# Loading the hashed rows with four DMAs a half, and turning them into dense columns

## What is computed

```python
xk = x + dxprev * time_maa_k
e_idx = token_ids.reshape(N).astype(jnp.int32) * HASH_PRIME % E
...
buf = jnp.zeros((E * C + 1, D), dtype=x.dtype).at[slot].set(xk_flat)
expert_in = buf[:E * C].reshape(E, C, D)
h = jnp.square(jax.nn.relu(jnp.einsum('ecd,edf->ecf', expert_in, w_key)))
expert_out = jnp.einsum('ecf,efd->ecd', h, w_value)
```

## Time and profile before

| | us |
|---|---|
| median of 3 runs | 2495.83 (2494.95 to 2498.03) |
| the profiled execution's own time | 2494.64 |
| its span in the profile | 2492.9 |
| hashed experts, from the first turn to the last product | about 1471 to 1852 of the span |
| granted TensorE clock, mean of the span | 0.993 |

### The profile page before, as it was taken

The page is one execution under the profiler, slowest core; times in us unless marked ns, Lnnn a source line. Parts: engine busy times, 40 slices in busy tenths (PEclk is TensorE's granted clock), DMA queues, the critical chain, the costliest instruction groups (busy, mean ns, idle before and its releaser), DMA issues.

```text
span 2492.9 us, 40630 instructions
## 1 busy us (share of the span) xinstructions
PE 2429.3 (97%) x12307; PEld 2021.7 (81%) x12309; DVE 1195.2 (48%) x1833; ACT 901.0 (36%) x1459; POOL 548.4 (22%) x498
## 2 busy tenths in 40 slices
PE   8999999999999899999999989999999999999999
PEld 4778888888899688888888868888888888888877
DVE  5555455325343243443444357777753333333356
ACT  3233333216555322222222236666652222222234
POOL 1100000002222266666666610000001111111100
PEclk9999999999999899999999999999999999999999
DMA  8698888407466533364345256666642111111135
GB/s 287 203 336 301 304 320 312 164 18 275 164 214 248 178 114 115 109 254 120 106 126 178 93 197 223 235 242 225 233 171 77 51 44 45 51 46 46 42 101 185
DMA packets 165172, 420.68 MB, mean 169 GB/s; under 512 B 31379, under 2 KB 67699, under 8 KB 148578
## 3 DMA queue, kind: packets, MB, share of 16 engines
q1 hardware_dynamic: 137810, 322.08, 37.2%
q0 software_dynamic: 19072, 61.66, 8.1%
q10 hardware_dynamic: 8208, 35.88, 3.8%
HBM read 558.71 MB, written 144.80 MB: 282 GB/s over the span
## 4 chain that ended last, share of the span: by engine, by line
PE 68%; DMA 2%; DVE 2%; issue 2%; ACT 1%; SPq 0%; POOL 0%; another core or an unknown queue 0%; DVEq 0%; POOLq 0%; ACTq 0%
PE s_g L99 8%; PE s_g L101 8%; PE s_g L100 8%; PE s_h_ps L99 5%; PE s_h_ps L101 5%; PE s_h_ps L100 5%; PE s_z_ps L99 2%; PE s_z_ps L101 2%; PE s_z_ps L100 2%; PE s_o_ps L99 2%; PE s_o_ps L100 2%; PE s_o_ps L101 1%; PE s_h L99 1%; PE s_h L100 1%; PE s_h L101 1%
## 5 line engine op out<-in xcount | busy, mean ns | idle before, releaser
L99 PE MATMUL s_g<-wx_hi,s_x_hi 128*128 128x512 f32 x512 | 203.3, 397 | 2.3 <-DVE s_x_lo L2339 1.6
L101 PE MATMUL s_g<-wx_hi,s_x_lo 128*128 128x512 f32 x512 | 199.8, 390 | 0.0
L100 PE MATMUL s_g<-wx_lo,s_x_hi 128*128 128x512 f32 x512 | 199.4, 390 | 0.0
L2234 POOL DMA_INDIRECT s_y<-mid_hash_out,first_rec x32 | 31.5, 985 | 736.0 <-DMA mid_hash_out<-s_o 392.7
L2045 DVE TENSOR_TENSOR s_w_lo<-s_w_raw,s_w_hi 128x1024 fp32r<-128x1024 f32 x124 | 146.4, 1221 | 46.6 <-ACT s_w_hi L1974 45.4
L99 PE MATMUL s_h_ps<-s_x_hi,s_w_hi 128*128 128x256 f32 x512 | 145.7, 285 | 7.1 <-DVE s_x_lo L2077 7.1
L99 PE MATMUL s_g<-s_u,s_c_hi 128*128 128x512 f32 x384 | 150.2, 391 | 1.6 <-PEq L1858 1.6
L101 PE MATMUL s_g<-s_u,s_c_lo 128*128 128x512 f32 x384 | 149.9, 390 | 0.0
L100 PE MATMUL s_g<-s_u,s_c_hi 128*128 128x512 f32 x384 | 149.4, 389 | 0.0
L101 PE MATMUL s_h_ps<-s_x_hi,s_w_lo 128*128 128x256 f32 x512 | 145.5, 284 | 0.0
L100 PE MATMUL s_h_ps<-s_x_lo,s_w_hi 128*128 128x256 f32 x512 | 145.5, 284 | 0.0
(11 more groups left out here) (411 smaller groups left out, 6747.3 us busy)
## 6 DMA issues: line engine op xcount, KB each, us to landing
s_half<-mid_w ACTq DMA_DIRECT2D x124, 2048.0 KB
s_w_raw<-in_w SPq DMA_DIRECT2D x64, 512.0 KB, 6.1
mid_w<-s_x_grp SPq DMA_DIRECT2D x32, 1024.0 KB, 5.8
mid_w<-s_pool_b SPq DMA_DIRECT2D x32, 1024.0 KB, 4.9
s_half<-mid_w SPq DMA_DIRECT2D x32, 1024.0 KB
s_w_raw<-in_w2h SPq DMA_DIRECT2D x16, 2048.0 KB, 9.1
s_w_raw<-in_w1h SPq DMA_DIRECT2D x15, 2048.0 KB, 7.5
mid_routed<-s_o_sb SPq DMA_DIRECT2D x72, 256.0 KB
```

The costliest lines, as they stand in the source:

```text
L99: pe.matmul(out, a_hi, w_hi, start=first, stop=False, skip_group_check=True)
L100: pe.matmul(out, a_hi, w_lo, start=False, stop=False, skip_group_check=True)
L101: return pe.matmul(out, a_lo, w_hi, start=False, stop=last, skip_group_check=True)
L2234: pool.indirect_dma_start(y[:], None, d["hash_out"], bass.IndirectOffsetOnAxis(rec[:, SLOTH:SLOTH + 1].bitcast(U32), 0)).then_inc(S["y_in" ...
```

## The change

The load of a half is written as four DMAs, one for each quarter of the channels, each into 32 partitions. Partition 32g + t now gets in its block s the quarter g of row 32s + t, where before it got row 4t + s. VectorE's turn of these blocks then writes the column 32s + t: 32 neighbouring columns for each block, where before each block went to every fourth column. All rows end in the same place as before. The wait of the turn counts 64 for each expert in place of 16. The recurrent stage keeps the old write pattern under the new name `turn_dealt_quarters`.

```diff
 def load_by_quarters(eng, dst, rows, sem):
 
-    eng.dma_start(dst, rows.rearrange("r (g c) -> g r c", c=P)).then_inc(sem, 16)
+    for g in range(P // 32):
+        eng.dma_start(dst[32 * g:32 * g + 32].rearrange("t (s c) -> t s c", c=P),
+                      rows[:, g * P:(g + 1) * P].rearrange("(s t) c -> t s c", t=32)).then_inc(sem, 16)
...
+def turn_dealt_quarters(dve, dst, src):
+
+    return dve.transpose(dst.rearrange("p k (t s) -> p k s t", s=4), src.rearrange("p (s k a) -> p k s a", s=4, a=32))
+
+
...
 def turn_quarters(dve, dst, src):
 
-    return dve.transpose(dst.rearrange("p k (t s) -> p k s t", s=4), src.rearrange("p (s k a) -> p k s a", s=4, a=32))
+    return dve.transpose(dst.rearrange("p k (s t) -> p k s t", t=32), src.rearrange("p (s k a) -> p k s a", s=4, a=32))
...
             def turn_x(m):
                 def stage(e):
-                    dve.wait_ge(S[f"x_in{m}"], e * 16 + 16)
+                    dve.wait_ge(S[f"x_in{m}"], e * 64 + 64)
                     wait_for(dve, S[f"x_lo{m}"], e)
                     turn_quarters(dve, xt[:, :, rows(m)], x[:, m]).then_inc(S[f"xt{m}"], 1)
...
-                turn_quarters(dve, tx_ps[:], y[:]).then_inc(S["tx"], 1)
+                turn_dealt_quarters(dve, tx_ps[:], y[:]).then_inc(S["tx"], 1)
```

## The result

The changed kernel takes 2483.39 us, the median of five runs (2482.61 to 2483.79), against 2495.83 before (2494.95 to 2498.03). The ratio is 0.9949, 95% interval 0.9934 to 0.9963: 9.2 to 16.5 us faster. The forecast was 2483.6. On another chip the same pair gave 2482.74 against 2495.65, ratio 0.9946 (0.9933 to 0.9960).

What follows compares the result with a forecast made beforehand. TensorE, busy 97% of the span, bounds the kernel, so only its stops give time back. Steady stop -10.35 and entrance -2.1 sum to -12.4 us, with the median offset rounded to 2483.6; range 2481.8 to 2489.0.

Steps and rivals of the forecast that it cites:

- The stop of 0.69 us an expert: TensorE in `down(0)` before k = 6 waits for ht_lo behind the turns; all returns for 15 experts, -10.35 us.
- the free 0.14: Lateness of the weight load at that stop, in us, that costs TensorE nothing; the rest costs one for one.
- The price of the turn: VectorE's turn with dense writes into SBUF takes 0.70 us, bounds 0.66 and 1.09, in place of about 1.09.
- The steady load: Eight 64 KB DMAs an expert on SP's queue, 0.66 us each, 5.3 us in all, hidden: cost 0.
- The entrance: First x load ahead of the hashed stage: TensorE starts at 1473.9 in place of 1476.07, -2.1 us.
- The turn unchanged: Rival: turn into SBUF stays at 1.09 us, only the entrance gains about 1.7, 2494.1 us; chance 0.07.
- The entrance lost: Rival: load issues eat the entrance's gain, 2485.1 us at 85 GB/s or 2487.7 at 1.19 a piece; chance 0.12.
- A new wait: Rival: part of the stop comes back as another wait, or the turn costs 0.85, 2487 us; chance 0.05.
- SP the bound: Rival: eight pieces stall on SP's full queue, w2 late for ScalarE from 1.76 us a piece, 2512 us; chance 0.04.

Runs made afterwards that it cites:

- third turn: Changed kernel with a third dense turn per expert behind the second, half 1 again into an unread staging slice: 2491.26 us against 2495.54, ratio 0.9985.
- the 16 KB pieces: Changed kernel with each quarter's DMA cut into four of 16 KB, sixteen a half: 2526.92 us against 2495.54, ratio 1.0124.
- the DMAs alone: Kernel before with four DMAs a half, rows dealt as before and the turn still stepping four columns: 2490.97 us against 2493.72, ratio 0.9991.
- the step of two: Changed kernel with rows dealt so the turn writes every second column, eight 32 KB DMAs a half: 2486.83 us against 2495.54, ratio 0.9966.
- the slow load: Changed kernel's dense turn, fed by four DMAs a half cut by rows into all 128 partitions: 2482.99 us against 2493.72, ratio 0.9960.
- the other order: Kernel before with the fourth h_lo put ahead of the two turns in VectorE's list: 2487.89 us against 2493.72, ratio 0.9977.

## Why the prediction was right

**The stop of 0.69 us an expert.** The place and the mechanism held: the wait for ht_lo is gone, and a third turn brings it back. The size was a little too large. 0.61 us came back, 23.33 to 22.72, not 0.69. I had h_lo 0.06 us late, inside the free 0.14. The runs with the fourth h_lo ahead of the turns in the changed kernel, which wait nowhere for it but in the last expert, still need 22.70. So 0.02 is a rest of the wait and 0.06 was never a loss: I priced the stop by the 0.233 us from one product to the next ahead of it, and `down` without a stop takes 10.96 us where with it it takes 11.59, 0.63 more. A block of work compared as a whole is the better yardstick. Over 15 experts the term was 10.35 and measured 9.2. This is the term of the sum that was mis-sized.

**The price of the turn.** Taken 0.70 from the reduction pair and the PSUM row, measured 0.686. The number was good, the ground for it only in part: the reduction has its step on the side that it reads, and the price per step in SBUF that I drew from it does not hold as put, since a step of two floats costs nothing (0.689 us). What the runs show is a price for a write step of four floats; they do not say what a read step costs. The turn's overlap was sized by the old turn's 0.14 us; two dense turns start 0.61 apart, so it is 0.08, and h_lo came at 1.22 and not at 1.12 us. That is the rest of 0.02.

**The steady load.** Cost 0 was right, the issues being cheaper still: 0.50 us each with register work (3.97 for eight) where I took 0.66 from L112, and 0.33 without it where L112 has 0.60. The traces show which shape costs what: a median of 0.32 to 0.33 us where source and destination are split in the same way, 32 rows outermost (the changed kernel, the 16 KB pieces), and 0.56 where neighbouring rows of DRAM go into one partition (the DMAs alone, the step of two) or the four quarters of a row go into 128 partitions (the slow load). Why is open. So the dealing of row 32s + t has a use of its own. That a half moves in a quarter of the time did not come: the eighth piece went out 3.4 us after the first and took about 2.0 to land, so 512 KB were there after some 5.4 us (an estimate from these two), where the second turn had to wait until 8.75 us after the first issue. Of these 5.4 us SP's issues take 3.4, so it is mostly they that now set the time.

**The entrance.** Forecast -2.1, measured -2.34 from the first issue on. The pieces were out at 1468.4, well before the stage was entered at 1470.85; the second turn then started as soon as the first allowed. The load alone gave 1.4 and the dense turn on the slow load 0.6. The whole comes out of the first of these: 1.41 from the load, 0.71 as both turns now follow each other at once (1.30 us in place of 2.01), and 0.22 as the stage is entered 6.18 us after the first issue, where in the run with the DMAs alone it was 6.40.

**The sum.** It was -12.4 and came to -11.1 in the spans. The stop's size takes 1.2 off the gain and the stretches outside the stage 0.2. A term that the sum did not have takes 0.4: in the first expert `up` took 13.54 us in place of 13.14, since TensorE's granted clock, after the idle time at the entrance, rose later. The entrance gave 0.2 more than forecast, and 0.3 remains that I do not account for. That the median fell nearly on the forecast, 2483.39 against 2483.6, is luck for 1.2 us: the median of before lay 1.2 us above its profiled execution, and that of after lay on it, which made good what the mechanism gave less. The low end of my own range, 2482.3, lies 0.8 below what its terms give (2495.83 - 10.35 - 2.4 = 2483.1).

**The rivals.** The turn unchanged: out by the groups. The entrance lost: out, though the step of two shows what 0.56 us an issue and twice the number do to it. A new wait: not in the changed kernel, but the other order in the kernel before brought one for w1_lo, which had about 0.8 us to spare. SP the bound: did not come, and the rival was built on the wrong link. I had named w2, with 4.6 us of cover and 9.4 us to landing. In the changed kernel w2 takes 7.5 us to land (median), so it has some 1.9 us more and breaks even near 2.0 us a piece and not at 1.76. x half 1 is due at the second turn, 15.0 us after the first issue; with the eighth issue 7c after the first and 2.2 us to landing that is c = 1.8. Both are estimates from the traces, and they lie near each other; that it is x that is late first, the 16 KB pieces show.

## What to carry to other kernels

Before a turn or another VectorE instruction is priced, look at the step of its writes in SBUF: with f32, steps of one and two floats cost the same and a step of four cost 0.40 us more on 512 columns, while a step of four into PSUM cost nothing; how rows are dealt at the load is free to choose and can make the writes dense. When a wait behind a block of work is found, look for all that stands behind the block, since a shorter block serves every one of them and another order only the one that is moved ahead. And count a queue's issues against the first consumer of the data they bring, not only against what is queued behind them.

## What was not expected of the hardware

- An issue of 64 KB costs SP 0.33 us in the changed kernel and 0.56 in the run with the DMAs alone, by the shape of the two sides: same bytes, same pieces of 512 bytes.
- The old form held SP up to 9.4 us in one issue and the store behind it 2.7. In the changed kernel 128 issues had a median of 0.33 and a maximum of 1.18 us. Eight DMAs an expert in a form that moves at 85 GB/s held SP up to 7.7 us in one issue, so it is not the number of DMAs.
- After the idle time at the entrance TensorE ran its first products of the stage at the lower level, mean granted clock 0.50 for the first 3 us in both kernels, in the changed one for some 0.4 us longer. In the run with 16 KB pieces it fell to that level inside the steady stage too, behind stops of 2.4 to 2.8 us, though not behind each of them.
